# The rectified key difference moves into the ring of score banks, with a new order of a TensorE turn

## What is computed

```python
xn = _layernorm(x, axis=-1)
qkv = (xn @ W_qkv + b_qkv).reshape(B, D, 3, H, p).transpose(2, 0, 3, 1, 4)
q, k, v = (qkv[0], qkv[1], qkv[2])
scores = jax.nn.softmax(jnp.einsum('bhip,bhjp->bhij', q, k), axis=-1)
out = jnp.einsum('bhij,bhjp->bhip', scores, v)
...
x = x + attention + y
```

## Time and profile before

| | us |
|---|---|
| median of 3 runs | 5298.06 |
| lowest and highest | 5297.58, 5298.85 |
| the profiled execution | 5298.86 |
| its span, first to last instruction | 5297.1 |
| mean granted TensorE clock, as a share | 0.996 |

### The profile page before, as it was taken

The page is one execution under the profiler, slowest core; times in us unless marked ns, Lnnn a source line. Parts: engine busy times, 40 slices in busy tenths (PEclk is TensorE's granted clock), DMA queues, the critical chain, the costliest instruction groups (busy, mean ns, idle before and its releaser), DMA issues.

```text
span 5297.1 us, 98782 instructions
## 1 busy us (share of the span) xinstructions
PE 5257.8 (99%) x36138; PEld 2253.0 (43%) x36138; DVE 4788.0 (90%) x9106; ACT 4948.1 (93%) x9746; POOL 826.5 (16%) x582
## 2 busy tenths in 40 slices
PE   8999999999999999999999999999999999999999
PEld 7433333333333333333333333333333333333798
DVE  7899999999999999999999999999999999996333
ACT  6799999999999999999999999999999999999544
POOL 3457773000000000000000000000000000000000
PEclk9899999999999999999999999999999999999999
DMA  7410110000000000000000000000000000000111
GB/s 240 155 37 31 49 53 21 13 13 10 13 13 13 11 7 13 13 13 13 10 13 13 13 11 6 13 13 13 13 10 13 13 13 12 6 13 10 36 48 36
DMA packets 212337, 139.93 MB, mean 26 GB/s; under 512 B 149280, under 2 KB 189088, under 8 KB 209312
## 3 DMA queue, kind: packets, MB, share of 16 engines
q1 hardware_dynamic: 208416, 110.83, 8.3%
q0 software_dynamic: 3456, 23.07, 1.2%
HBM read 88.75 MB, written 42.99 MB: 25 GB/s over the span
## 4 chain that ended last, share of the span: by engine, by line
ACT 42%; PE 41%; issue 8%; DVE 5%; ACTq 0%; DVEq 0%
ACT probs L878 35%; PE psum L1163 15%; PE psum L1125 13%; PE psum L1149 7%; ACT spill L894 7%; PE psum L1265 3%; PE psum L1250 3%; DVE maxima L951 3%; DVE o_t L990 1%; DVE merged L947 0%; DVE probs L960 0%; PE psum L1104 0%; DVE maxima L947 0%; DVE maxima L960 0%; PE psum L1182 0%
## 5 line engine op out<-in xcount | busy, mean ns | idle before, releaser
L878 ACT ACTIVATE probs<-psum 128x512 f32<-128x512 f32 x8192 | 4265.6, 627 | 70.1 <-PE psum L1149 37.6
L951 DVE TENSOR_REDUCE maxima<-psum 128x1 f32<-128x512 f32 x6042 | 3869.4, 683 | 161.0 <-PE psum L1125 120.1
L1149 PE MATMUL psum<-q_rows,k_rows 50*128 50x512 f32 x8192 | 2327.1, 481 | 0.0
L1125 PE MATMUL psum<-k_halves,q_halves 48*128 48x512 f16 x7049 | 2192.7, 386 | 4.9 <-DVE maxima L947 0.7
L1163 PE MATMUL psum<-probs,v_cols 128*17 128x512 f32 x16384 | 2158.3, 599 | 3.7
L1149 PEld LDWEIGHTS psum<-q_rows,k_rows 50*128 50x128 f32 x8192 | 1297.0, 187 | 139.0 <-ACT probs L878 64.9
L1125 PEld LDWEIGHTS psum<-k_halves,q_halves 48*128 48x128 f16 x7049 | 526.2, 93 | 1406.1 <-DVE maxima L947 826.2
L947 DVE CUSTOM_DVE_ANT_0 merged<-psum,spill 128x512 bf16<-128x512 f32 x1007 | 689.4, 685 | 2.7 <-issue 2.7
L782 POOL TENSOR_TENSOR o_t<-o_t,recip 128x256 f32<-128x256 f32 x64 | 39.7, 620 | 3911.2 <-DVE recip L994 3911.2
L894 ACT ACTIVATE spill<-psum 128x512 f32<-128x512 f32 x1007 | 629.0, 625 | 9.6 <-PE psum L1125 4.0
L1163 PEld LDWEIGHTS psum<-probs,v_cols 128*17 128x17 f32 x16384 | 272.9, 95 | 497.9 <-issue 418.5
(11 more groups left out here) (133 smaller groups left out, 2366.8 us busy)
## 6 DMA issues: line engine op xcount, KB each, us to landing
q_halves<-q_parts SPq DMA_DIRECT2D x384, 64.0 KB, 2.3
k_halves<-k_parts SPq DMA_DIRECT2D x192, 64.0 KB, 2.3
planes<-in_up_planes POOLq DMA_DIRECT2D x10, 1024.0 KB, 5.2
planes<-in_down_planes POOLq DMA_DIRECT2D x10, 1024.0 KB, 5.0
y<-in_x SPq DMA_DIRECT2D x16, 512.0 KB, 4.3
xn_transposed<-xnt SPq DMA_DIRECT2D x16, 512.0 KB, 5.2
q_parts<-parts SPq DMA_DIRECT2D x32, 256.0 KB, 5.5
k_parts<-parts SPq DMA_DIRECT2D x32, 256.0 KB, 3.3
```

The source lines that it names most:

```text
L878: nc.scalar.activation(probs[:, 2 * (u % 2) + half, BANK * g:BANK * g + BANK], ps_s[:, r % 4, :], ACT.Exp).then_inc(s_exp, 1)
L951: nc.vector.tensor_reduce(largest, region(use), axis=AX_X, op=ALU.max).then_inc(s_region_free, 1)
L1125: nc.tensor.matmul(region(use_of[n, j]), q_halves[lower:lower + ROWS, m % 2, P * t:P * t + P], keys[lower:lower + ROWS, :], start=True, st ...
L1149: nc.tensor.matmul(ps_s[:, r % 4, :], k_rows[s // 2 % 2][lower:lower + ROWS + MAX_PARTS, key:key + P], q_rows[s % 2][lower:lower + ROWS + ...
```

## The change

The difference leaves the region banks and takes a place in ACT's ring of four score banks: positions 0 to 3 of a turn are scores 0 to 3, position 4 is the difference, positions 5 to 8 are scores 4 to 7, and position k of 9 uses bank k modulo 4. The regions (banks 4 to 6) then have 7 uses in a turn. The order in which PE does a turn is new, pieces and scores have other halves, and the merged piece is the one after the difference. The difference is now of the keys of chunks 3 and 7 of a row (half 1 less half 0, chunk 3 of each); it was of chunks 6 and 7.

```diff
-        DIFF_FROM, DIFF_TO = IN_ROW - 2, IN_ROW - 1
+        DIFF_FROM, DIFF_TO = IN_ROW // 2 - 1, IN_ROW - 1
...
-                            nc.vector.tensor_tensor(k_kept[:, k, :], k_kept[:, k, :], ps_qk[:, m, :], ALU.subtract).then_inc(s_diff, 1)
+                            nc.vector.tensor_tensor(k_kept[:, k, :], ps_qk[:, m, :], k_kept[:, k, :], ALU.subtract).then_inc(s_diff, 1)
...
-        PIECE = [(1, 0), (1, 1), (0, 0), (1, 2), (0, 1), (0, 2), (1, 3), (0, 3)]
-        DIFFERENCE, MERGED = 3, 6
+        PIECE = [(1, 0), (1, 1), (0, 0), (1, 3), (0, 3), (1, 2), (0, 1), (0, 2)]
+        DIFFERENCE, MERGED = 3, 4
...
-        SCORE = [(r // 2 % 2, 2 * (r // 4) + r % 2) for r in range(2 * QG)]
+        SCORE = [(0, 0), (0, 1), (1, 0), (1, 1), (1, 2), (0, 2), (0, 3), (1, 3)]
...
-                elif n + 1 < TILES_ALL:
+                elif n + 1 < AHEAD:
                     use((n + 1, j), False)
...
+        RING = 2 * QG + 1
+
+        def score_bank(u, r):
+            return ps_s[:, (RING * u + r + (r >= QG)) % 4, :]
+
+        def difference_bank(n):
+            return ps_s[:, (RING * (n - AHEAD) + QG) % 4, :] if n >= AHEAD else region(use_of[n, DIFFERENCE])
...
# in piece(n, j)
-                    free_region(use_of[n, j])
+                    if j != DIFFERENCE or n < AHEAD:
+                        free_region(use_of[n, j])
+                    else:
+                        pe.wait_ge(s_exp, 2 * QG * (n - AHEAD) + 1)
...
# in score(u, r)
-                    if e >= 4:
+                    if r < QG and u > 0:
                         pe.wait_ge(s_exp, e - 3)
+                    if QG <= r < 2 * QG - 1:
+                        pe.wait_ge(s_exp, e - 2)
+                    if r == 2 * QG - 1 and u + AHEAD < TILES_ALL:
+                        pe.wait_ge(s_spilled, spilled(u + AHEAD))
+                    if r == 2 * QG - 1 and u + AHEAD >= TILES_ALL:
+                        pe.wait_ge(s_exp, 2 * QG * u + 1)
...
# the turn
+                    score(u + 1, 0)
                     piece(n, 0)
-                    score(u + 1, 0)
+                    score(u + 1, 1)
                     piece(n, 1)
-                    score(u + 1, 1)
                     score(u + 1, 2)
+                    score(u + 1, 3)
                     piece(n, 2)
-                    score(u + 1, 3)
                     sums(u, 0)
                     piece(n, 3)
+                    score(u + 1, 4)
                     piece(n, 4)
-                    score(u + 1, 4)
+                    piece(n, 5)
                     score(u + 1, 5)
-                    piece(n, 5)
+                    piece(n, 6)
                     score(u + 1, 6)
                     score(u + 1, 7)
-                    piece(n, 6)
                     piece(n, 7)
                     sums(u, 1)
```

More of the change, by code:

```diff
@@ L878, in exp @@
                     nc.scalar.activation(probs[:, 2 * (u % 2) + half, BANK * g:BANK * g + BANK],
-                                         ps_s[:, r % 4, :], ACT.Exp).then_inc(s_exp, 1)
+                                         score_bank(u, r), ACT.Exp).then_inc(s_exp, 1)
                 def rectify_pair(n, i):
@@ L893, in rectify @@
                         act.wait_ge(s_region_free, vector_uses[use_of[n - 2, MERGED]])
-                    nc.scalar.activation(spill[:, n % 2, :], region(use_of[n, DIFFERENCE]), ACT.Relu).then_inc(s_spilled, 1)
+                    nc.scalar.activation(spill[:, n % 2, :], difference_bank(n), ACT.Relu).then_inc(s_spilled, 1)
                 nc.scalar.activation(warm[0:1, 1:2], one[0:1, 0:1], ACT.Exp)
@@ L1123, in piece @@
                     keys = k_diff[at] if j == DIFFERENCE else k_halves[:, at, BANK * chunk:BANK * chunk + BANK]
-                    free_region(use_of[n, j])
-                    nc.tensor.matmul(region(use_of[n, j]), q_halves[lower:lower + ROWS, m % 2, P * t:P * t + P],
+                    if j != DIFFERENCE or n < AHEAD:
+                        free_region(use_of[n, j])
+                    else:
+                        pe.wait_ge(s_exp, 2 * QG * (n - AHEAD) + 1)
+                    nc.tensor.matmul(difference_bank(n) if j == DIFFERENCE else region(use_of[n, j]), q_halves[lower:lower + ROWS, m % 2, P * t:P * t + P],
                                      keys[lower:lower + ROWS, :], start=True, stop=True)\
@@ L1145, in score @@
                         pe.wait_ge(s_neg_in, 2 * 16 * (s + 1))
-                    if e >= 4:
+                    if r < QG and u > 0:
                         pe.wait_ge(s_exp, e - 3)
+                    if QG <= r < 2 * QG - 1:
[4 more added lines that the diff above has]
+                        pe.wait_ge(s_exp, 2 * QG * u + 1)
                     lower, key = HALF_P * half, P * (u % UNITS)
-                    nc.tensor.matmul(ps_s[:, r % 4, :], k_rows[s // 2 % 2][lower:lower + ROWS + MAX_PARTS, key:key + P],
+                    nc.tensor.matmul(score_bank(u, r), k_rows[s // 2 % 2][lower:lower + ROWS + MAX_PARTS, key:key + P],
                                      q_rows[s % 2][lower:lower + ROWS + MAX_PARTS, BANK * g:BANK * g + BANK],
```

## The result

The changed kernel takes 5591.5 us (median of 4 runs, 5588.4 to 5592.3), the kernel before 5297.8: a ratio of 1.055 (95% interval 1.054 to 1.0565), 294 us slower. Forecast were 5510 us and a range from 5355 to 5560. The direction and the mechanism were right; the size fell short (212 of the 294 us), and the time lies outside the range.

The account below looks back on a forecast made before the run. DVE's piece-4 reduction, closely followed by ACT's rectification and PE, bounded the turn. Legs of 1.02 + 0.98 + 1.78 + 0.98 = 4.76 us against 4.535 gave +226 us over 1005 turns, less 14: 5510 us, range 5355 to 5560.

Parts of the forecast that it names:

- The bound before: Before the sums of half 1, DVE's piece-4 reduction and ACT's rectification paths end nearly together, DVE's later by 0.06 us.
- the leg: PE's stretch from the difference to the start of the sums of half 1: 1.53 us before, 1.78 us forecast.
- The keys, and the copies of the first block: DVE copies kept keys at chunks 3 and 11 instead of 6 and 14 in the first block: no cost.
- The difference in ACT's ring: Score 7 takes over piece 6's wait for the rectification; by this wait the sums of half 1 start 0.04 us later.
- The first rival: Array halves report completions separately, so ACT's path through rectification and score 7 sets 4.60 us a turn: 5363 us; chance 0.12.
- Score 4 ahead of piece 4: In PE's turn after the difference, piece 4 is reported behind score 4, so DVE learns of it 0.25 us later.
- The choice of the upper end: For piece 4's late report, a price between 0 and 0.25 us: 0.25 taken, assuming completions reported in program order.
- So DVE starts piece 4 at 0.64 + 0.07 after the difference: DVE's piece-4 reduction starts 0.71 us after the difference: 0.64 for score 4's end, 0.07 from matmul end to DVE's start.
- The first leg: From score 0 to the sums of half 0 on PE: 1.02 us in every turn, against 1.02 and 1.07 before.
- The late reports of pieces 0 to 2: Pieces 0 to 2 are reported behind a score, about 0.1 us late; DVE has idle time for it.
- The change of block swallowed in part: Of 0.055 us a turn lost around block changes, DVE's added idle time swallows a quarter, 14 us in all.
- The upper bound, 5560: Top of the range: 0.05 us a turn more than forecast, for late reports of pieces 0 to 2.

Follow-up runs that it names:

- both mends: The changed kernel with piece 4 ahead of score 4 again and DVE waiting for the rectification one reduction earlier, ahead of piece 2: 5353.2 us (1.0103).
- The last run: The kernel before, with DVE waiting for the rectification one reduction ahead of the merged one: 5324.6 us (1.005).
- the old banks: The kernel before, its banks kept, with the changed kernel's halves of the scores and score 4 ahead of piece 4: 5469.8 us (1.0324).
- the early wait: The changed kernel with DVE waiting for the rectification ahead of piece 2, one reduction before the merged one: 5477.1 us (1.0334).
- the ring alone: The kernel before with nine uses on ACT's four score banks, its order, keys and halves unchanged: 5586.7 us (1.0541).
- piece 4 first: The changed kernel with piece 4 moved ahead of score 4 again, all else as changed: 5371.7 us (1.0135).

## Why the prediction was right or wrong

- **The bound before.** Right. The two loops, through DVE's reduction of piece 4 and through ACT's rectification, are what set the turn; each one reappears alone in a run (DVE's in the changed kernel, ACT's with both mends). The last run adds that the leg between them isn't free of DVE either: 0.07 us on the reduction of piece 5 cost 0.025 us a turn.
- **The keys, and the copies of the first block.** Costed at nothing; 5296.7 against 5299.0 us. Right.
- **The difference in ACT's ring: the wait comes back in score 7.** Right: 295 us of waits before a score where 288 stood before a piece. The first rival's time for ACT's loop, 4.60 us a turn, came out at 4.61 once DVE's loop was out of the way.
- **Score 4 ahead of piece 4, 0.25 us on the leg.** Right in mechanism, and nearly in size: 0.22 us on the leg in the old banks (1.53 to 1.75), 0.22 on DVE's start in the new ones. The choice of the upper end, a report in program order, was right. By the Trainium skill (TensorE: Matmul & The Clock Gate, Part 3, The mechanism) matmuls keep program order in start and end. These runs agree on what it says of ends: piece 4's semaphore is raised 0.03 us after score 4's and never before. The records disagree on starts: in the turn of the earlier trace rows piece 5 starts at 2010.50, after scores 6 and 7 that follow it in the program (four scores in the 1.11 us from 2009.84). What the runs can't tell is whether piece 4 itself ends late or is only reported late, since the ends in a trace are modelled.
- **The step that failed: "So DVE starts piece 4 at 0.64 + 0.07 after the difference".** That took the 0.07 from the plain reduction of the earlier trace rows for an instruction that the change makes a merged one, with two waits. I had the merged piece's new place in the diff, and had costed that part at nothing without saying so. Measured 0.79 in place of 0.71. The foreseen part came out at 0.68 (a plain reduction in the old banks, and the merged one with the early wait), for score 4's semaphore is raised 0.63 us after the difference and DVE starts 0.05 us later; the second wait adds 0.11, worth 114 us on the chip. With them the sum would have been 5510 + 1005 x 0.08 = 5590.
- **The first leg, 1.02 us.** 1.01. Right. The late reports of pieces 0 to 2, if there are any, cost nothing.
- **The change of block swallowed in part.** I took a quarter of 0.055 us a turn. The mean is 4.88 and the quiet turn 4.85, so nearly half was swallowed.
- **The upper bound, 5560.** It held 0.05 us a turn for late reports of other pieces and nothing for the start of the merged reduction, the one term with no row of its own: no merged reduction in the rows had waited for its piece.

What stays open: whether piece 4 ends late or is reported late, and whether the 0.11 us belong to a second wait as such or to the piece's wait standing in an instruction of its own.

No version beats the kernel before. The best that does all the work with this ring, the one with both mends, takes 1.010 of its time. Nine uses on four banks make the last score before the sums wait for the fourth use before it, which is the rectification; in the kernel before it waits for exp 3, one place earlier in ACT's order, and a shorter fp16 piece takes the wait instead. The order of the turn in the kernel before is the better one.

## What to carry to other kernels

When an instruction is moved between two others of PE's program, count for the consumers of those behind it too: here a score of 0.57 us, ahead of a piece in the other half of the array, delayed the piece's reader by 0.22 us, and in a closed loop that is paid in every turn. A wait that is taken off one instruction (the rectification, off piece 6) is not gone until you have found no other that meets it; with one use more in a ring, every waiter looks one place later. What stands behind that waiter in the same rows of the array is late with it, as piece 6 behind score 7 in the ring alone (0.23 us a turn). And where an instruction is given the place after an idle stretch, price its own start there: with a second wait, for something long done, it was 0.11 us later.

## What the runs showed of the hardware beyond what was expected

- A DVE reduction with two waits starts later than one with a single wait, though the second was met long ago: 0.79 against 0.68 us after the difference, and 0.57 against 0.46 with piece 4 first. The trace has a semaphore instruction of its own ahead of such a reduction. On piece 5's reduction in the kernel before two waits cost 0.07 us (0.73 against 0.66 on the mean), and where DVE had other work nothing that shows (0.61 in both).
- The matmuls of the two halves of the array raise their semaphores in program order: that of the fp16 piece behind a score came 0.03 us after the score's, 0.66 us after the difference, in the changed kernel, in that with the early wait and in the old banks with score 4 first; ahead of the score it came at 0.44. The piece's record starts at the same place in all of them.
